# A four-layer graph network on one core: matmuls of zeros in TensorE's waits, records scattered in pairs, 39 row buffers, and a border that is merged

## The chip, the core and the metric

The kernel runs on one core of one Trainium2 chip, as one program. Times are microseconds of device time (us). The core's engines are TensorE (PE, with its weight loads as PEld), VectorE (DVE), ScalarE (ACT), GpSimd (POOL) and SyncE (SP). Each has a queue of its own and works in its order; they meet at semaphores. SP, ACT and POOL issue DMAs.

## What is computed

384 nodes with 512 features pass through four layers; each has a part on the graph (12,288 edges) and a part on the nodes, each added to its input:

```
x = x + L0_gnn(ln(x))   # softmax over a dense 8 x 384 x 384 matrix of edge weights, times values, elu, layer norm
x = x + L0_ffn(ln(x))   # each node's first expert by a gate, with gelu
x = x + L1_gnn(ln(x))   # 4 blocks: sparse attention by segments, then relu(y @ m_w1) @ m_w2
x = x + L1_ffn(ln(x))   # top-2 of 16 experts, 96 places each
x = x + L2_gnn(ln(x))   # graph attention: exp of a score per edge, sum of weighted rows by node
x = x + L2_ffn(ln(x))   # 8 experts mixed by a softmax
x = x + L3_gnn(ln(x))   # transformer attention on the graph
x = x + L3_ffn(ln(x))   # one of 3 attentions is chosen by argmax(relu(mean(x) @ r_w1 + b) @ r_w2 + b)
```

In L0 the weights are `softmax(mat)`, and `y = matmul(softmax(mat), x @ Wv + bv)` by head (8 heads of 64 columns). The tables of edges have to be sorted by node for L2, which is done once, on the chip.

## The kernel before

N = 384 nodes are NT = 3 tiles of P = 128 rows; D = 512 columns are KC = 4 chunks. Each engine has one hand-written queue: functions marked `@on("pe")`, `@on("dve")` and so on are run in the order of the text. No planner changes it. TensorE writes to eight banks of PSUM in turn: `banks.open` (line 54) waits until the bank's last user has freed it and gives the bank, `banks.filled` and `banks.drained` are the readers' and the writers' waits. A `mm` (line 372) of fp32 operands is two records of the trace.

The places that the change touches, in the order of time:

- **The bucket's start** (lines 893 to 902). TensorE turns the first rows (`l0x`), waits until they are drained, then for `bucket_ready` from VectorE, and multiplies two small triangles.
- **The softmax of L0** (lines 999 to 1030 on PE, 1073 to 1095 on ACT, 1403 to 1495 on DVE). `l0o0` to `l0o2` are the values, copied by ACT to `ost`. `totals` is a small matmul that DVE reads. `chunk_max_by_halves(2)` takes the row maxima of the last third of the matrix (`wm[2]`), after which ACT makes 24 exponentials (8 heads, 3 tiles), each with its row sum by `accum_out`. TensorE turns the weights of a head (line 1012, 9 transposes) and multiplies them with `ost`; `head_out` scales by the reciprocals of the sums.
- **The edges' scatter** (lines 2125 to 2135). POOL writes ST = 104 columns of records to `tab_sorted` by indirect DMAs, behind the banks `base0`, `base1`, ..., which TensorE fills during L1. `few_underway` (line 291) waits, before each, for the landing of the one two places ahead. TensorE, DVE and ACT work on the blocks of L1 meanwhile; their results meet at line 2061.
- **L1's experts** (lines 2184 to 2375). A gate (`f1g`), the count of places (`f1p1`, `f1n1`, `f1p2`), rows scattered to `tab_x`; ACT loads them group by group (`load_group`, 384 rows in one DMA), TensorE turns them (line 2248) and runs the 16 experts; DVE copies all results (line 2362), ACT stores them in `tab_eo`.
- **L2's start** (lines 2425 to 2445 on PE, 2500 to 2510 on ACT). Rows of `tab_eo` are gathered and added, normed (`act_row_std`), turned and multiplied.
- **The rows of L2.** POOL gathers 98 rows of 128 x 512 by `pool_scatter_rows` (line 629) to GR = 31 buffers, at most four underway. The first 31 are issued while the scores of the edges are made; then come the lanes (`lanes_ready` 1 to 5, small steps between DVE and PE), and then the sums, in which a buffer is free when TensorE has used it (`msg_used`).
- **L2's mixer, L3's choice and the end.** `f2g` (line 2713); `f3x`, the mean of each column by `accum_out` (line 3061), `f3r`, `f3g` and `q_taken`; after the last `f3y` one DMA of x to `out` by SP (line 3161), released by `out_ready`.

## Time and profile before

| | us |
|---|---|
| median of 3 runs | 1850.32 (1849.62 to 1850.44) |
| the profiled execution | 1841.83 |
| its span | 1840.1 |
| PE busy | 1601.8 (87%) |
| DVE, ACT, POOL busy | 886.2, 501.0, 645.1 |
| mean granted clock of TensorE | 0.925 |

The clock is given as a share of full speed: 1.00 is 2.4 GHz, 0.50 is 1.2 GHz. An engine that is busy for 87% of the span can still wait where others set the end, and part of its busy time is work at the lower clock. The chain of waits is the path that ended last, followed back.

### The profile page before, as it was taken

Reading aid. Unit: us, or ns where it says so; the run is one execution under the profiler, and the core shown is the slowest. Engines: PE = TensorE matmul, PEld = TensorE weight load, DVE = VectorE, ACT = ScalarE, POOL = GpSimd, SP = SyncE. Lnnn points to the kernel's source line nnn. Section 1 sums busy time; section 2 is a strip of 40 time slices with the busy share of each in tenths; the row PEclk is TensorE's granted clock in tenths of the full one; section 3 lists DMA queues with packets and bytes.
Section 4 is the critical chain, followed back from the end, with each engine's and each line's share of the span. In section 5 each row is a group of like instructions: output and inputs, shape, how many; then the busy total and the mean of one; then the engine's idle time right before and its main releaser. Section 6 shows DMA issues by size and latency. Waiting matters only on the chain.

```text
span 1840.1 us, 22730 instructions
## 1 busy us (share of the span) xinstructions
PE 1601.8 (87%) x6886; PEld 886.1 (48%) x6916; DVE 886.2 (48%) x2166; ACT 501.0 (27%) x1608; POOL 645.1 (35%) x756
## 2 busy tenths in 40 slices
PE   5989999997798999996995976488699899999698
PEld 3534444446454555463553745333244455555455
DVE  8878888887624524432353154576632101011322
ACT  1134444446422324141231214211110211111233
POOL 5867787862322335453002613457300000000000
PEclk9999999998698999997997886589899999999899
DMA  7021101007223132321216734346315122211020
GB/s 305 12 96 24 58 24 59 24 12 202 40 91 117 51 100 53 88 76 33 92 46 134 277 97 143 99 126 178 125 56 202 69 74 68 97 47 34 6 63 17
DMA packets 119547, 161.71 MB, mean 88 GB/s; under 512 B 49433, under 2 KB 61657, under 8 KB 119090
## 3 DMA queue, kind: packets, MB, share of 16 engines
q1 hardware_dynamic: 93024, 115.43, 20.2%
q0 software_dynamic: 18592, 29.91, 6.0%
q10 hardware_dynamic: 7858, 15.44, 2.5%
q8 instruction: 41, 0.67, 0.2%
q14 instruction: 32, 0.26, 0.1%
HBM read 145.26 MB, written 15.47 MB: 87 GB/s over the span
## 4 chain that ended last, share of the span: by engine, by line
PE 78%; DVE 12%; another core or an unknown queue 3%; issue 3%; ACT 2%; DMA 1%; POOL 0%; DVEq 0%; ACTq 0%; POOLq 0%
PE psum L373 76%; DVE stats L464 1%; DVE arena L2622 1%; DVE ring L1281 1%; PE psum L1012 1%; DVE xn L2042 1%; DVE xn L2048 0%; PE psum L2248 0%; DVE xn L2061 0%; DVE ring L656 0%; DVE mv L465 0%; PE psum L398 0%; DMA x<-in_x 0%; POOL tab_x L2291 0%
## 5 line engine op out<-in xcount | busy, mean ns | idle before, releaser
L373 PE MATMUL psum<-arena 128*128 128x128 f32 (+9 forms) x1814 | 328.9, 338 | 57.9 <-issue 31.7
L373 PE MATMUL psum<-arena,ring 128*128 (+1 forms) x1478 | 322.8, 363 | 9.0 <-issue 6.2
L373 PE MATMUL psum<-xT,ring 128*128 128x384 f32 x928 | 321.2, 508 | 9.8 <-ACT ring L3068 4.2
L373 PEld LDWEIGHTS psum<-arena 128*128 128x128 f32 (+5 forms) x1814 | 201.0, 157 | 191.7 <-issue 117.2
L373 PE MATMUL psum<-ring,arena 128*128 128x512 f32 (+1 forms) x592 | 273.4, 610 | 14.0 <-issue 6.6
L373 PE MATMUL psum<-ring,xT 128*128 128x512 f32 x552 | 250.5, 606 | 4.0 <-DMA bc<-in_wide 2.9
L373 PEld LDWEIGHTS psum<-xT,ring 128*128 128x128 f32 x928 | 183.2, 199 | 141.4 <-issue 31.4
L373 PEld LDWEIGHTS psum<-arena,ring 128*128 128x128 bf16 (+1 forms) x1504 | 139.2, 115 | 130.0 <-issue 28.6
L373 PEld LDWEIGHTS psum<-ring,arena 128*128 128x128 f32 (+1 forms) x592 | 103.4, 189 | 140.8 <-issue 139.4
L1063 ACT ACTIVATE ring<-ring 128x128 f32<-128x128 f32 x416 | 123.3, 297 | 173.1 <-DVE ring L1347 168.6
L373 PEld LDWEIGHTS psum<-ring,xT 128*128 128x128 f32 x552 | 104.3, 194 | 125.3 <-issue 119.9
L844 POOL DMA_INDIRECT tab_bucketed<-rec,pos x96 | 95.6, 996 | 186.2 <-DMA tab_bucketed<-rec,pos 178.3
L1347 DVE SCALAR_TENSOR_TENSOR ring<-psum,wa 128x1024 f32<-128x1024 f32 x104 | 127.4, 1225 | 59.5 <-PE psum L373 58.9
L2132 POOL DMA_INDIRECT tab_sorted<-rec,pos x104 | 100.4, 965 | 87.7 <-DMA tab_sorted<-rec,pos 62.0
L1155 POOL TENSOR_SCALAR arena<-iota,arena 128x128 bf16<-128x128 f32 x200 | 122.0, 619 | 15.0 <-DVE xT L1361 11.8
L1167 POOL DMA_INDIRECT tab_w<-xT,pair x104 | 109.9, 1057 | 49.2 <-DMA tab_w<-xT,pair 32.4
L408 ACT ACTIVATE arena<-psum 128x384 f32<-128x384 f32 (+1 forms) x133 | 63.6, 500 | 192.7 <-PE psum L373 154.1
L2061 DVE TENSOR_TENSOR xn<-xn,psum 128x512 f32<-128x512 f32 x24 | 16.5, 687 | 139.3 <-PE psum L373 106.4
L621 POOL DMA_INDIRECT ring<-tab_h,sd_t x72 | 74.6, 1037 | 24.7 <-issue 16.2
L482 ACT ACTIVATE std<-mv,eps_col 128x1 f32<-128x1 f32 x57 | 16.8, 294 | 227.9 <-DVE mv L465 203.6
L1063 ACT ACTIVATION_READ_ACCUMULATOR ring<-ring 128x1 f32 x416 | 77.6, 186 | 0.0
L1355 DVE TENSOR_REDUCE mask_dst<-ring 128x4 f32<-128x512 f32 x104 | 70.3, 676 | 0.0
(468 smaller groups left out, 1632.6 us busy)
## 6 DMA issues: line engine op xcount, KB each, us to landing
ring<-in_L_ffn_w SPq DMA_DIRECT2D x22, 1024.0 KB, 6.6
ring<-in_L_gnn_m_w SPq DMA_DIRECT2D x8, 1024.0 KB
ring<-in_L_ffn_expert_weights SPq DMA_DIRECT2D x8, 1024.0 KB
ring<-tab_key ACTq DMA_DIRECT2D x24, 256.0 KB
ring<-in_L_gnn_Wv SPq DMA_DIRECT2D x5, 1024.0 KB, 5.2
tab_w<-xn SPq DMA_DIRECT2D x6, 768.0 KB, 14.6
ring<-in_L_gnn_Ww SPq DMA_DIRECT2D x4, 1024.0 KB, 7.7
ring<-in_L_gnn_wq SPq DMA_DIRECT2D x4, 1024.0 KB, 5.8
```

Source lines behind the costliest of these rows:

```text
L373: return nc.tensor.matmul(o, a, b, start=start, stop=stop)
L408: nc.scalar.activation(dst, b[:, 0:w], ACT.Copy).then_inc(banks.free_of(name), 1)
L464: od.link(nc.vector.bn_stats(stats[:, t, :], src[:, t, :]))
L621: return nc.gpsimd.indirect_dma_start(o, None, table, bass.IndirectOffsetOnAxis(ap=column.bitcast(U32), axis=0), **more)
L844: nc.gpsimd.indirect_dma_start(tab_bucketed, bass.IndirectOffsetOnAxis(ap=pos[:, q:q + 1].bitcast(U32), axis=0), rec[:, q, :], None).then_ ...
L1012: last = nc.tensor.transpose(b[:, t * P:(t + 1) * P], weights_of(h, t)[:, c * P:(c + 1) * P], ident[:])
L1063: last = nc.scalar.activation(prod2[:, b % 2, h, :], prod2[:, b % 2, h, :], ACT.Copy, accum_out=w_sum[:, b, h:h + 1])
L1155: last = nc.gpsimd.tensor_scalar(edge_is[:, j, k, s_, :], iota[:, 0:P], key_rq[:, s_, T:T + 1], None, ALU.is_equal)
L1167: nc.gpsimd.indirect_dma_start(tab_w, bass.IndirectOffsetOnAxis(ap=pair[:, q:q + 1].bitcast(U32), axis=0), w_edge0[:, q, :], None).then_in ...
L1347: V.scalar_tensor_tensor(out=prod2[:, b % 2], in0=z_bank[:, b % 2], scalar=0.0, in1=wa_all, op0=ALU.max, op1=ALU.mult).then_inc(z_free, 1)
L1355: V.tensor_reduce(w_sum[:, b, 0:H8 // 2], prod2[:, b % 2, 0:H8 // 2, :], AX, ALU.add).then_inc(halves_summed, 1)
L2132: nc.gpsimd.indirect_dma_start(tab_sorted, bass.IndirectOffsetOnAxis(ap=pos2[:, q:q + 1].bitcast(U32), axis=0), rec[:, q, :], None).then_i ...
```

## The change

A function `keep_clock(b, n, w)` is added: n fp32 matmuls of a block of zeros (128 x w, w is 256 or 128), each into the bank b, which TensorE has opened and fills next, and whose content is overwritten. It is called 19 times, ahead of waits of TensorE, with counts of 3 to 22. Beside it:

- In L0 the totals' matmul moves ahead of `l0o2`, and `chunk_max_by_halves(2)` ahead of DVE's reading of the totals. `accum_out` goes from the exponentials; `ost` gets a column of ones for each head, so that the product's 65th column is the row sum; the reciprocal and its product move to `head_out`.
- SP waits for the landing of the halves of `wm[2]` before it loads the base rows.
- The scatter to `tab_sorted` waits for two landings before every second record (`OF_RECORDS` is 2), in place of one before each.
- The first group of `tab_x` comes in three DMAs and is turned tile by tile. The last 5 results of the 16 are copied by ACT, the first 11 by DVE, which then makes all of `l2_fold`.
- L2: ACT's order of stds and turned blocks; GR is 39 (the new buffers are parts of `xT`, `xT2` and `xn2`) with eight shared semaphores; during the first 39 rows POOL waits at every sixth for the landing of the four before.
- L3: the column means by 12 matmuls against ones in a bank `f3m` and a sum on DVE, ACT's four copies around `f3r`, their drain behind the choice.
- The output leaves in three DMAs, each behind its `f3y`.

The diff, without lines that only serve names (each hunk's head stands, its unchanged lines do not):

```diff
@@ -23,7 +23,7 @@
-GR = 31
+GR = 39
@@ -372,6 +372,10 @@
+        def keep_clock(b, n, w=256):
+            for _ in range(n):
+                mm(b[:, 512 - w:512], zeros[:, 0:P], zeros[:, 0:w], True, True)
+
@@ -596,9 +600,10 @@
-        ost = view(NT * N * H8, NT, D)
-        pw = view(NT * N * H8 + NT * D, 2, NT - 1, N)
-        pw_flat = view(NT * N * H8 + NT * D, N * H8 // 2)
+        ost = view(NT * N * H8, NT, H8 * (HD + 1)).rearrange("p t (h d) -> p t h d", h=H8)
+        after_ost = NT * N * H8 + NT * H8 * (HD + 1)
+        pw = view(after_ost, 2, NT - 1, N)
+        pw_flat = view(after_ost, N * H8 // 2)
@@ -607,6 +612,8 @@
+        go_rows += [v.rearrange("p c n -> p (c n)")[:, k * D:(k + 1) * D] for v, ks in ((xT, (0, 1, 2)), (xT2, (0, 2))) for k in ks]
+        go_rows += [xn2[:, t, :] for t in range(NT)]
@@ -621,10 +628,11 @@
+        ROW_GROUP = 6
-            earlier = 1 if T % GR < 2 * NT else RECORDS + ST // UN if T % GR >= GR - UN else 0
-            eng.wait_ge(rows_landed[T % GR], 16 * (earlier + T // GR + 1))
+            earlier = 1 if T % UN < 2 * NT else 0
+            eng.wait_ge(rows_landed[T % UN], 16 * (earlier + T // UN + 1))
@@ -632,9 +640,12 @@
-                if T >= ROWS_UNDERWAY:
+                if 0 < T < GR and T % ROW_GROUP == 0:
+                    for k in range(max(T - ROWS_UNDERWAY, 0), T):
+                        row_landed(pool, k)
+                elif T >= ROWS_UNDERWAY:
-                pool_gather(go_rows[T % GR], table, sd_t[:, T:T + 1]).then_inc(rows_landed[T % GR], 16)
+                pool_gather(go_rows[T % GR], table, sd_t[:, T:T + 1]).then_inc(rows_landed[T % UN], 16)
@@ -893,8 +904,9 @@
+            b = banks.open(pe, "bucket")
+            keep_clock(b, 6)
-            b = banks.open(pe, "bucket")
@@ -999,15 +1011,20 @@
-            pe.wait_ge(totals_ready, 1)
-            b = banks.open(pe, "totals")
-            mm(b[:, 0:NT], tri[:], node_total, True, True)
-            mm(b[:, 16:16 + NT], ones[:], node_total, True, True).then_inc(banks.full_of("totals"), 1)
+                if t == 1:
+                    pe.wait_ge(totals_ready, 1)
+                    b = banks.open(pe, "totals")
+                    mm(b[:, 0:NT], tri[:], node_total, True, True)
+                    mm(b[:, 16:16 + NT], ones[:], node_total, True, True).then_inc(banks.full_of("totals"), 1)
-                    pe.wait_ge(exp_done, h + 1)
+                    if h > 0:
+                        pe.wait_ge(exp_done, h + 1)
+                        if h == 0 and c == 0:
+                            keep_clock(b, 6)
+                            pe.wait_ge(exp_done, 1)
@@ -1073,8 +1090,7 @@
-                                            bias=gate[:, 5, t * H8 + h:t * H8 + h + 1],
-                                            accum_out=gate[:, 9, h * NT + t:h * NT + t + 1])
+                                            bias=gate[:, 5, t * H8 + h:t * H8 + h + 1])
@@ -1083,8 +1099,11 @@
-            for t in range(NT):
-                act_copy(act, f"l0o{t}", ost[:, t, :])
+            nc.scalar.activation(ost[:, :, :, HD], ones[:, 0:NT * H8].rearrange("p (t h) -> p t h", t=NT), ACT.Copy)
+            for t in range(NT):
+                b = banks.filled(act, f"l0o{t}")
+                nc.scalar.activation(ost[:, t, :, 0:HD], b.rearrange("p (h d) -> p h d", h=H8),
+                                     ACT.Copy).then_inc(banks.free_of(f"l0o{t}"), 1)
@@ -1423,11 +1442,11 @@
+            chunk_max_by_halves(2)
-            chunk_max_by_halves(2)
@@ -1461,9 +1480,11 @@
-                b = banks.filled(dve, f"l0y{h}")
-                V.tensor_tensor(xn2[:, :, h * HD:(h + 1) * HD], b[:, 0:NT * HD].rearrange("p (t d) -> p t d", t=NT),
-                                gate[:, 9, h * NT:(h + 1) * NT].unsqueeze(2).broadcast_to([P, NT, HD]),
+                b = banks.filled(dve, f"l0y{h}")[:, 0:NT * (HD + 1)].rearrange("p (t d) -> p t d", t=NT)
+                s3 = gate[:, 9, h * NT:(h + 1) * NT]
+                od.link(V.reciprocal(s3, b[:, :, HD]))
+                od.link(V.tensor_tensor(s3, s3, keep.rearrange("p (t h) -> p h t", h=H8)[:, h, :], ALU.mult))
+                V.tensor_tensor(xn2[:, :, h * HD:(h + 1) * HD], b[:, :, 0:HD], s3.unsqueeze(2).broadcast_to([P, NT, HD]),
@@ -1689,6 +1706,8 @@
+            sp.wait_ge(w_loaded[0], 32)
+            sp.wait_ge(w_loaded[NT - 1], 16)
@@ -1704,6 +1723,7 @@
+                keep_clock(bk["f0x"][0], *((14,) if t == 0 else (5, P)))
@@ -1875,8 +1895,12 @@
+                        if (k, i, c, t) == (0, 0, 0, 0):
+                            keep_clock(bk[0], 15, P)
+                if (k, i) == (0, 0):
+                    keep_clock(bk[0], 11, P)
@@ -2128,7 +2152,9 @@
-                few_underway(pool, q, RECORDS, OF_RECORDS)
+                if q >= OF_RECORDS and q % OF_RECORDS == 0:
+                    for k in range(q - OF_RECORDS, q):
+                        pool.wait_ge(ranks_landed[k % UN], 16 * (RECORDS + k // UN + 1))
@@ -2151,6 +2177,7 @@
+        ACT_RESULTS = 11
@@ -2184,6 +2211,10 @@
+            def load_first_group():
+                for t in range(NT):
+                    act.dma_start(xrows[:, t, :], tab_x[t * P:(t + 1) * P, :]).then_inc(first_group[t], 16)
+
@@ -2192,12 +2223,18 @@
+            def take_result(e):
+                act.wait_ge(results_stored[e % GE], 16 * (e // GE))
+                b = banks.filled(act, f"f1e{e}")
+                nc.scalar.activation(eo[0:CAP1, e % GE, :], b[0:CAP1, :], ACT.Copy).then_inc(banks.free_of(f"f1e{e}"), 1)
+                store_result(e)
+
-            load_group(0)
+            load_first_group()
@@ -2209,10 +2246,11 @@
-                if e >= 2:
+                if 2 <= e < ACT_RESULTS + 2:
-            for e in range(E1 - 2, E1):
-                store_result(e)
+                if e > ACT_RESULTS:
+                    take_result(e - 1)
+            take_result(E1 - 1)
@@ -2223,25 +2261,38 @@
-            def before(name, mask):
-
-                b = banks.open(pe, name)
+            def before(b, name, mask):
+
+            b = banks.open(pe, "f1p1")
+            keep_clock(b, 5)
-            before("f1p1", chosen_1)
+            before(b, "f1p1", chosen_1)
+            b = banks.open(pe, "f1p2")
+            keep_clock(b, 8)
-            before("f1p2", chosen_2)
+            before(b, "f1p2", chosen_2)
-                pe.wait_ge(group_in[g % 2], 16 * (g // 2 + 1))
+                if g == 0:
+                    bk = [banks.open(pe, f"f1t0{c}") for c in range(KC)]
+                    keep_clock(bk[0], 22)
+                    for t in range(NT):
+                        pe.wait_ge(first_group[t], 16)
+                        for c in range(KC):
+                            last = nc.tensor.transpose(bk[c][:, t * P:(t + 1) * P], xrows[:, t, c * P:(c + 1) * P], ident[:])
+                            if t == NT - 1:
+                                last.then_inc(banks.full_of(f"f1t0{c}"), 1)
+                    return
+                pe.wait_ge(group_in[g % 2], 16 * (g // 2 if g % 2 == 0 else g // 2 + 1))
@@ -2355,13 +2406,14 @@
-            for e in range(E1):
+            for e in range(ACT_RESULTS):
-                if E1 - GE - 1 <= e < E1 - 1:
-                    l2_fold(dve, od, e - (E1 - GE - 1))
+            for j in range(GE):
+                l2_fold(dve, od, j)
+            banks.filled(dve, f"f1h{E1 - 1}")
@@ -2429,6 +2481,7 @@
+            keep_clock(ends, 22)
@@ -2470,28 +2523,33 @@
-            pe.wait_ge(lanes_ready, 1)
+                if k == 0:
+                    keep_clock(b, 9)
+                    pe.wait_ge(lanes_ready, 1)
+            b = banks.open(pe, "l2m")
+            keep_clock(b, 6)
-            b = banks.open(pe, "l2m")
+            b = banks.open(pe, "l2w")
+            keep_clock(b, 3)
-            b = banks.open(pe, "l2w")
+                b = banks.open(pe, f"l2v{k}")
+                keep_clock(b, (6, 3)[k])
-                b = banks.open(pe, f"l2v{k}")
@@ -2500,8 +2558,11 @@
-            for t in range(NT):
+            act_row_std(act, ROW_L2, 0)
+            act_turned_block(act, "l2x", xT, 0)
+            for t in range(1, NT):
+            for t in range(1, NT):
@@ -2711,6 +2772,7 @@
+            keep_clock(logits, 13)
@@ -2983,10 +3045,22 @@
-            pe_transpose_rows(pe, "f3x", xn, 6 * NT)
+            bk = [banks.open(pe, f"f3x{c}") for c in range(KC)]
+            means = banks.open(pe, "f3m")
+            for t in range(NT):
+                if t == NT - 1:
+                    keep_clock(means, 7)
+                pe.wait_ge(row_ready, 6 * NT + t + 1)
+                for c in range(KC):
+                    last = mm(means[:, c * NT + t:c * NT + t + 1], xn[:, t, c * P:(c + 1) * P], ones[:, 0:1], True, True)
+                if t == NT - 1:
+                    last.then_inc(banks.full_of("f3m"), 1)
+                for c in range(KC):
+                    last = nc.tensor.transpose(bk[c][:, t * P:(t + 1) * P], xn[:, t, c * P:(c + 1) * P], ident[:])
+                    if t == NT - 1:
+                        last.then_inc(banks.full_of(f"f3x{c}"), 1)
-            for c in range(KC):
-                banks.drained(pe, f"f3x{c}")
+            banks.drained(pe, "f3m")
@@ -3016,12 +3090,16 @@
+            for c in range(KC):
+                banks.drained(pe, f"f3x{c}")
+            b = banks.open(pe, "f3q0")
+            keep_clock(b, 7)
-                pe_cols(pe, f"f3q{c}", xT, w, c * P)
+                pe_cols(pe, f"f3q{c}", xT, w, c * P, b=b if c == 0 else None)
@@ -3056,11 +3134,12 @@
-            for c in range(KC):
-                b = banks.filled(act, f"f3x{c}")
-                nc.scalar.activation(xT[:, c, :], b[:, 0:N], ACT.Copy, accum_out=route[:, c:c + 1]).then_inc(banks.free_of(f"f3x{c}"), 1)
+            for c in range(KC // 2):
+                act_copy(act, f"f3x{c}", xT[:, c, :], N)
+            for c in range(KC // 2, KC):
+                act_copy(act, f"f3x{c}", xT[:, c, :], N)
@@ -3102,6 +3181,8 @@
+            b = banks.filled(dve, "f3m")[:, 0:KC * NT].rearrange("p (c t) -> p c t", c=KC)
+            nc.vector.tensor_reduce(route[:, 0:KC], b, AX, ALU.add).then_inc(banks.free_of("f3m"), 1)
@@ -3157,9 +3235,10 @@
-            sp.wait_ge(out_ready, 1)
-            sp.dma_start(tiled(out), x[:]).then_inc(stored, 16)
-            sp.wait_ge(stored, 16)
+            for t in range(NT):
+                banks.drained(sp, f"f3y{t}")
+                sp.dma_start(out[t * P:(t + 1) * P, :], x[:, t, :]).then_inc(stored, 16)
+            sp.wait_ge(stored, 16 * NT)

```

On TensorE, at the start of the heads of L0, the order before (`gate,tri` is the totals, `ident,ring` a transpose of the first head):

```order
L373 MATMUL psum<-ring,xT 128x512 [waits bank_free2]
L373 MATMUL psum<-ring,xT 128x512 x3
L373 MATMUL psum<-rows,ones 128x512
L373 MATMUL psum<-gate,tri 128x3 [waits bank_free3,totals_ready]
L373 MATMUL psum<-gate,ones 128x3
L1012 MATMUL psum<-ident,ring 128x128 [waits bank_free4,exp_done]
L1012 MATMUL psum<-ident,arena 128x128 x2
L1012 MATMUL psum<-ident,ring 128x128 [waits bank_free5]
L1012 MATMUL psum<-ident,arena 128x128 x2
```

and now, from the second of the values on:

```order
L373 MATMUL psum<-ring,xT 128x512 [waits bank_free1]
L373 MATMUL psum<-ring,xT 128x512 x3
L373 MATMUL psum<-rows,ones 128x512
L373 MATMUL psum<-gate,tri 128x3 [waits bank_free2,totals_ready]
L373 MATMUL psum<-gate,ones 128x3
L373 MATMUL psum<-ring,xT 128x512 [waits bank_free3]
L373 MATMUL psum<-ring,xT 128x512 x3
L373 MATMUL psum<-rows,ones 128x512
L373 MATMUL psum<-zeros 128x256 [waits bank_free4]
L373 MATMUL psum<-zeros 128x256 x5
L1029 MATMUL psum<-ident,ring 128x128 [waits exp_done]
L1029 MATMUL psum<-ident,arena 128x128 x2
```

The totals stand ahead of the third `ring,xT`, and six products of zeros ahead of the wait for the exponentials.

On GpSimd, at the start of the scatter to the sorted table (`rec` are the records, `pos` their places), before:

```order
L2132 DMA tab_sorted<-rec,pos 26112x4 [waits bank_free7,sorted_cleared,bucketed_loaded]
L2132 DMA tab_sorted<-rec,pos 26112x4
L2132 DMA tab_sorted<-rec,pos 26112x4 [waits ranks_landed0]
L2132 DMA tab_sorted<-rec,pos 26112x4 [waits ranks_landed1]
L2132 DMA tab_sorted<-rec,pos 26112x4 [waits ranks_landed2]
```

and now:

```order
L2158 DMA tab_sorted<-rec,pos 26112x4 [waits bank_free7,sorted_cleared,bucketed_loaded]
L2158 DMA tab_sorted<-rec,pos 26112x4
L2158 DMA tab_sorted<-rec,pos 26112x4 [waits ranks_landed1,ranks_landed0]
L2158 DMA tab_sorted<-rec,pos 26112x4
L2158 DMA tab_sorted<-rec,pos 26112x4 [waits ranks_landed3,ranks_landed2]
```

Each record waited for one landing; now every second one waits for two, and the one behind it for none.

On TensorE, between L1's gate and its experts, before (`arena` in the transposes is the first group of rows):

```order
L373 MATMUL psum<-gate,tri_b 128x16 [waits bank_free2,step_ready]
L373 MATMUL psum<-gate,ones_b 128x16
L373 MATMUL psum<-gate,tri_b 128x16
L373 MATMUL psum<-gate,ones_b 128x16 x2
L373 MATMUL psum<-gate,tri_b 128x16
L2248 MATMUL psum<-ident,arena 128x128 [waits bank_free3,group_in0]
L2248 MATMUL psum<-ident,arena 128x128 x2
L2248 MATMUL psum<-ident,arena 128x128 [waits bank_free4]
```

and now:

```order
L373 MATMUL psum<-zeros 128x256 x7
L373 MATMUL psum<-gate,tri_b 128x16 [waits step_ready]
L373 MATMUL psum<-gate,ones_b 128x16
L373 MATMUL psum<-gate,tri_b 128x16
L373 MATMUL psum<-gate,ones_b 128x16 x2
L373 MATMUL psum<-gate,tri_b 128x16
L373 MATMUL psum<-zeros 128x256 [waits bank_free5,bank_free6,bank_free4,bank_free3]
L373 MATMUL psum<-zeros 128x256 x21
L2291 MATMUL psum<-ident,arena 128x128 [waits first_group0]
L2291 MATMUL psum<-ident,arena 128x128 x3
L2291 MATMUL psum<-ident,arena 128x128 [waits first_group1]
L2291 MATMUL psum<-ident,arena 128x128 x3
```

Ahead of each of the two waits stand products of zeros, and the transposes wait by tile for a load of their own.

## Rows read from the trace of the kernel before

**Rows 1.** Page, part 4: shares of the chain that ended last, by engine

```profile
PE 78%; DVE 12%; another core or an unknown queue 3%; issue 3%; ACT 2%; DMA 1%; POOL 0%; DVEq 0%; ACTq 0%; POOLq 0%
```

**Rows 2.** TensorE by stretch: start:end, length, busy us (instructions), granted clock, DMA share, GB/s

```profile
433.00:453.00 20.00, 20.00 (x185) 1.00 0.21 66
...
1014.00:1024.00 10.00, 8.88 (x44) 0.53 0.17 66
1093.90:1102.00 8.10, 7.32 (x17) 0.51 0.13 36
1118.00:1186.00 68.00, 38.97 (x564) 0.53 0.50 154
...
1746.30:1750.40 4.10, 4.08 (x7) 0.51 0.69 155
```

**Rows 3.** Three blocks of layer 1 by stretch: PE, PEld, DVE, ACT, POOL busy, clock

```profile
673.70:745.80 72.10, 70.35 (x257) 40.47 (x257) 29.07 (x58) 24.58 (x58) 36.61 (x38) 1.00 0.28 70
773.10:862.97 89.87, 72.95 (x257) 41.49 (x257) 29.17 (x59) 24.83 (x58) 45.44 (x47) 0.90 0.22 59
891.95:963.40 71.45, 70.05 (x256) 40.49 (x257) 29.07 (x58) 24.79 (x58) 0.00 (x0) 1.00 0.18 59
```

**Rows 4.** Chain of waits, 812 to 856 and 1100 to 1210: start, us, what

```profile
819.35 31.63 another core or an unknown queue
...
1131.12 7.89 another core or an unknown queue
```

**Rows 5.** GpSimd in time: start, us, line, operation, count [idle before it <-releaser]

```profile
641.42 0.96 POOL L844 DMA_INDIRECT tab_bucketed<-rec,pos  x1 [1.39 <-DMA tab_bucketed<-rec,pos]
...
818.32 0.96 POOL L2132 DMA_INDIRECT tab_sorted<-rec,pos  x1 [0.30 <-issue]
...
850.60 0.96 POOL L2132 DMA_INDIRECT tab_sorted<-rec,pos  x1 [0.30 <-issue]
```

**Rows 6.** All engines in time, 415 to 434

```profile
420.87 0.16 DVE L1427 COPY gate<-psum 128x3 f32<-128x3 f32 x1 [4.43 <-PE psum L373]
...
425.76 1.00 ACT L1075 ACTIVATE arena<-ring,gate 128x384 f32<-128x384 f32 x1 [3.68 <-DVE gate L1412]
...
427.88 0.47 PE L1012 MATMUL psum<-ident,ring 128*128 128x128 f32 x1 [7.04 <-ACT arena L1075]
```

**Rows 7.** TensorE in time, 10 to 24

```profile
16.58 0.17 PE L373 MATMUL psum<-gate,tri_b 128*128 128x9 bf16 x1 [3.49 <-DVE gate L1206]
```

**Rows 8.** What TensorE waited for: us in total, times, longest

```profile
PE psum L398 <- DVE xn L477: 15.5, 3, 12.7
PE psum L2248 <- DMA arena<-tab_x: 12.9, 1, 12.9
```

**Rows 9.** TensorE and ScalarE in time, 1093 to 1108

```profile
1100.03 1.99 PE L373 MATMUL psum<-ring,xT 128*128 128x512 f32 x2
...
1101.99 1.10 PE L373 MATMUL psum<-ring,xT 128*128 128x512 f32 x2
...
1105.42 0.66 PE L398 MATMUL psum<-ident,xn 128*128 128x128 f32 x4 [1.72 <-DVE xn L477]
...
1104.24 0.28 ACT L482 ACTIVATE std<-mv,eps_col 128x1 f32<-128x1 f32 x1
```

**Rows 10.** GpSimd's gathers of rows in time, first and last of 67

```profile
1208.91 1.14 POOL L621 DMA_INDIRECT arena<-tab_h,sd_t  x1 [30.67 <-PE psum L373]
...
1303.41 0.95 POOL L621 DMA_INDIRECT arena<-tab_h,sd_t  x1 [0.30 <-issue]
```

**Rows 11.** All engines in time, 1729 to 1747

```profile
1739.60 1.84 PE L373 MATMUL psum<-route,ring 128*128 128x1 f32 x8 [1.65 <-ACT xT L3061]
...
1746.32 0.98 PE L373 MATMUL psum<-xT,ring 128*128 128x384 f32 x1 [4.22 <-ACT ring L3068]
```

**Rows 12.** The output's DMA (issue to landing), and the chain at a store of 192 KB

```profile
DMA to landing us min/median/max: 3.5/3.5/3.5
...
1082.67 2.06 DMA tab_eo<-arena
```

18 lines of the change are left out of this document (6 added, 12 removed).

## The prediction

> **What bounds the kernel now.** I read the chain of waits first: TensorE is 78% of it, VectorE 12%, and "another core or an unknown queue" 3% [rows 1], which on one core should be nothing and has to be explained. Then TensorE by stretch, for the granted clock: 0.53 of full speed in the experts' first transposes, 0.51 behind the gathers of L2's start, 0.53 through all 68 us in which L2's edges are scored [rows 2]. In each of these the engine had waited for others just before, or waits often. So the time is set by TensorE's work, by its waits, and by the work that runs at 1.2 GHz behind a wait. What a cold stretch costs can be read: a pair of 128x512 records lasts 1.99 us at the low clock and 1.10 at the full one [rows 9], and since the records of a pair overlap, a product of zeros of 256 columns costs half of what a 512-column product takes from start to start, near 0.45 us at full clock and 0.85 at half.
>
> The unknown 3% comes next. Three blocks of layer 1 hold the same work, but take 72.1, 89.9 and 71.5 us [rows 3]. In the long one the chain has a piece of 31.63 us of unknown from 819.35 on [rows 4], while VectorE waits for a product of TensorE. Exactly then GpSimd issues its scatters without a pause, one per 1.27 us from 818.32 to 850.60 [rows 5]; the piece ends at 850.98. In the third block GpSimd does nothing and no such piece exists. My reading: TensorE's signal reaches the waiting engine only when GpSimd's run of indirect DMAs has ended.
>
> **The change part by part.** All against the profiled execution's own 1841.8 us.
>
> *Scatter in pairs.* Each pair now ends with a wait for the later landing. Where GpSimd waited for the DMA just issued, starts lay about 2.36 us apart (0.96 of issue and 1.39 of idle time) [rows 5], and the chain has no unknown piece there. A pair then takes 1.27 + 2.36 = 3.6 us against 2.5, and the run is cut into pieces of 1.3 us. If a signal gets through in each pause, the middle block falls from 89.9 to 72, which is -17.9; I take -16, for some delay remains. The scatter's end moves: 104 records at 1.8 us are 189 us, about what it took, and the 27 left at 818 need 49 us and not 34, to 867. Its reader, the load of the sorted table, is a layer later. Bounds -18 and +12, the second if a signal still waits for the whole run, now 15 us longer.
>
> *L0's softmax.* VectorE is idle for 4.43 us ahead of the totals at 420.87 [rows 6]. The maximum of the last third moves there, so the exponentials no longer wait for VectorE (3.68 us in the same rows) but for ACT's own copies, some 1 us more: the start of the heads, 427.88, moves 3 us. Its first 5 us run at the low clock; six products of zeros (2.7 us, of a gap of 7.04) keep it up, worth about 2.5. Against that stand a 65th column and, behind the last head, a reciprocal and a product, +1.3. Sum -4.2, bounds -5.5 and -1.
>
> *The bucket's keep_clock.* This stands after the drain of `l0x`, at about 13.6, and TensorE is cold: 6 x 0.85 = 5.1 us reach to 18.7, where the product started at 16.58 [rows 7]. VectorE's long chain waits for it: +2.2, bounds 0 and +2.3. It is the one place where the zeros are longer than the wait.
>
> *L1's experts.* The transposes waited 12.9 us for their load [rows 8]; then 10 us ran at 0.53 [rows 2]. Twenty-two products are 9.9 us at full clock and fit; cold they would be 18.7 and late by 6. Five and eight products stand before it and bring the clock up, the first of them ending about 1 us late. With full clock 10 us at 0.53 lose 4.4 us, and turning tile by tile leaves a third of the transposes behind the last landing, another 1. With the late start: -3, bounds -6 and +6.
>
> *L1's end and L2's start.* Results 11 to 15 leave by ACT, with no `l2_fold` in front: 0.6 us earlier. The wait of 12.7 us [rows 8] takes 22 products of zeros (9.9 us), and 8.1 us at 0.51 behind it [rows 2] lose up to 3.5. The third std stood behind a copy, at 1104.24, so TensorE waited 1.72 us at 1105.42 [rows 9]; in the new order it doesn't. Up to -5.8; I take -4, bound +6 as above.
>
> *Rows of L2.* Between the first and last of 67 gathers lie 94.5 us, 1.43 each [rows 10]; TensorE waits for them here. Eight rows more are there beforehand: 8 x 1.43 = 11.5. What falls away turns cold TensorE at the end. But eight rows (1.25 each, as [rows 5]) and some four pauses of up to 2.4 lengthen GpSimd's part in the scoring by up to 20 us, beside which VectorE and TensorE exchange signals; there a run of eight gathers had an unknown piece of 7.89 us [rows 4], and runs are now cut at six. I set both at nothing and take -9 for the rows. Bounds -16 and +8.
>
> *L3's choice.* ACT's four copies with their sums lay ahead of the route's product: it waited 1.65 us and ran cold for 1.84 [rows 11]; now only a sum on VectorE lies there: -2.3. Seven products of zeros fill 3 of the 4.22 us before 1746.32 [rows 11], and 4.1 us at 0.51 [rows 2] become 2.1. -4, bounds -5 and -2.
>
> *The output.* A DMA of 768 KB took 3.5 us to land; one of 192 KB 2.06 [rows 12]. The last third, with the hop over VectorE's memset gone: -1.1. The Trainium skill, DMA: Bandwidth & Descriptors, "Anatomy of one DMA", fits 2.0 us plus bytes over 436 GB/s: 3.8 and 2.6 us by it, so the term would be -1.4.
>
> *The other zeros* (f0x, the first rows of layer 1, the lanes, `f2g`): each returns half of some 4 to 5 us of cold work if it fits its wait. I take -4.7 for all, bounds -10 and +3.
>
> Sum: -16 - 4.2 + 2.2 - 3 - 4 - 9 - 4 - 1.1 - 4.7 = -43.8. That gives 1798.0 on the profile's scale. The profiled execution lay 8.5 below the median of the runs, so the median should be 1806.5.
>
> One rule speaks against the zeros in L0. In the rows the clock is full through the later heads, 433 to 453 [rows 2], though a third of each head's time is transposes. The Trainium skill, TensorE: Matmul & The Clock Gate, "PE-mode transpose", says that transposes don't count as busy for the gate. By it the clock could fall again inside the heads, and the term would be 2.5 less; the trace doesn't bear that out.
>
> **The rivals.**
> - *The stall stays.* Pairs of issues might hold signals as runs do, the pause of about 1.4 us being too short; the two unknown pieces above don't show which pause frees them. The term -16 becomes 0: 1822. For it: the scoring stage has such pieces with runs of only eight; against it: none stood where single scatters had pauses.
> - *The zeros run cold.* The clock is down where they start, so they take twice as long: the two blocks of 22 end 6 us late each, and the gains at full clock (some 14 us) go. -43.8 + 25 gives 1831. For it: the clock before the experts' wait was low already. Against: five and eight products stand before the first of the two, and in [rows 9] the clock came back within unbroken work.
> - *Slower: signals are held for all of GpSimd's issuing, paused or not.* Then the longer scatter costs 12 and doesn't save 16 (+28), and 39 rows with pauses, ending near 1198, hold the lanes that began at 1186 (+12) and add some 6 to the scoring: 1806.5 + 46 = 1852. It decides at one point: whether TensorE's signals pass in a pause of one landing.
> - *More than forecast.* Cutting the gathers at six also frees the scoring, where the unknown pieces such as that of 7.89 sum to about 20: half of it gives 1796.
>
> **How the numbers follow.** The forecast 0.56; the stall stays 0.14; zeros cold 0.10; slower 0.08; more than forecast 0.12. The range, 1787 to 1836, leaves out the slower case and the tails of the outer two. A measurement of this kernel can tell about 0.2% (3.7 us) from no change. Faster by more: 0.90; within: 0.03; slower: 0.07, nearly all from the third rival, whose lower half would lie within.
>
> **What would show it.** The middle block of layer 1 at about 72 us, with no unknown piece near 820; if there is one as long as the scatter, the first or third rival holds. The granted clock near 1.00 behind the two waits of 12 us, and the zeros there at 0.43 to 0.47 each; at 0.85 the second. The bucket's product at about 18.7. The heads of L0 from 425. Gathers after the lanes: 59, with the same spacing. The forecast is wrong if the scoring stage grows beyond its 68 us, or if the rows' last gather comes no earlier relative to the lanes.

## The result, and the profile after

The changed kernel takes 1805.09 us (median of 4 runs, 1804.19 to 1807.99), the kernel before 1849.97 (4 runs, 1843.08 to 1850.44): a ratio of 0.9769, with a 95% interval of 0.9743 to 0.9794. Faster, by 2.3%. The profiled execution of after took 1805.19 us, so it lies on its median, where that of before (1841.83) lay 8.1 below the median of its four. Trace against trace the gain is 36.6 us, and 44.9 by the medians.

TensorE's busy time rose, though the span fell (page of after, part 1):

```profile
PE 1656.8 (92%) x7256; PEld 940.3 (52%) x7286; DVE 880.0 (49%) x2161; ACT 501.5 (28%) x1586; POOL 645.3 (36%) x756
```

55 us more. The new products (173, two records each) are nearly all of a group of 362 records and 89.7 us; other work got shorter at the full clock (group of the page: line, engine, form, count | busy, mean ns | idle before).

```profile
L373 PE MATMUL psum<-zeros 128*128 128x256 f32 (+3 forms) x362 | 89.7, 409 | 14.6 <-ACT cnt_dst L412 4.0 <-issue 3.1 <-DVE arena L2674 2.5
```

The three blocks of layer 1, by stretch (columns as in [rows 3]). The middle one takes 69.8 us in the place of 89.9; each stretch holds the same work, in 252 to 258 matmul records:

```profile
667.60:739.70 72.10, 70.68 (x258) 40.97 (x259) 29.74 (x59) 25.44 (x60) 26.96 (x28) 1.00 0.27 70
766.40:836.20 69.80, 69.14 (x252) 40.05 (x252) 27.42 (x56) 24.19 (x56) 28.43 (x30) 1.00 0.25 68
865.20:936.70 71.50, 70.08 (x257) 40.54 (x257) 29.19 (x58) 24.84 (x58) 27.23 (x28) 1.00 0.20 64
```

GpSimd in time, from 817 on (to be read against [rows 5]): two scatters 1.26 us apart, then 1.87 us of waiting.

```profile
817.96 0.96 POOL L2158 DMA_INDIRECT tab_sorted<-rec,pos  x1 [1.88 <-DMA tab_sorted<-rec,pos]
819.22 0.96 POOL L2158 DMA_INDIRECT tab_sorted<-rec,pos  x1 [0.30 <-issue]
822.05 0.96 POOL L2158 DMA_INDIRECT tab_sorted<-rec,pos  x1 [1.87 <-DMA tab_sorted<-rec,pos]
```

Not all of these waits are so short: in the middle block there are 14, of 2.6 us on average. And the wait of VectorE that was the piece of 31.63 us before now takes 14.0 us. "Remote" is the profile's word for a wait that ended long after the last recorded instruction that could have ended it. (VectorE in time, before; then what GpSimd and VectorE waited for in the middle block, after.)

```profile
851.01 0.69 DVE L2061 TENSOR_TENSOR xn<-xn,psum 128x512 f32<-128x512 f32 x1 [31.66 <-remote]
```

```profile
POOL tab_sorted L2158 <- DMA tab_sorted<-rec,pos: 36.8, 14, 4.9
...
DVE xn L2085 <- PE psum L373: 14.4, 3, 14.0
```

So some 14 of the 31.6 us were TensorE's own work on the product, and some 17.7 the lateness of its signal.

Start of L0's heads and the bucket's product, in time (for [rows 6] and [rows 7]). The zeros of L0 run from 422.20, 12 records in 2.86 us, and the first transpose starts at 425.85; those of the bucket took 2.83:

```profile
13.55 2.83 PE L373 MATMUL psum<-zeros 128*128 128x256 f32 x12 [0.67 <-ACT xT L412]
16.27 0.18 PE L373 MATMUL psum<-gate,tri_b 128*128 128x9 bf16 x1
...
422.20 2.86 PE L373 MATMUL psum<-zeros 128*128 128x256 f32 x12
...
425.85 0.33 PE L1029 MATMUL psum<-ident,ring 128*128 128x128 f32 x1 [0.80 <-ACT arena L1092]
```

TensorE's waits from 985 to 1110 (for [rows 8]): that for the loads of `tab_x` is 1.7 us and not 12.9. Behind both long waits the clock is now full (TensorE by stretch, columns as in [rows 2]), but it is 0.54 in the scoring, as before:

```profile
PE psum L2291 <- DMA arena<-tab_x: 1.7, 2, 1.0
...
986.00:996.00 10.00, 7.23 (x57) 1.00 0.41 129
1062.20:1070.30 8.10, 6.54 (x30) 1.00 0.15 47
1084.60:1151.00 66.40, 40.90 (x534) 0.54 0.50 152
```

And the place where the gain did not come. What VectorE waited for in the sums, 1165 to 1292, and the chain there:

```profile
DVE arena L652 <- PE psum L373: 16.7, 8, 7.8
DVE arena L652 <- remote: 15.1, 1, 15.1
...
1242.95 15.06 another core or an unknown queue
...
1283.93 6.66 another core or an unknown queue
```

The two pieces are not alike. Ahead of the end of the first, TensorE is idle for 13.58 us while GpSimd issues gathers to 1254.76: that is a late signal. In the second TensorE works without a pause to 1290.35, and GpSimd issues nothing: that is TensorE's own work, though the profile finds no releaser for its end. (GpSimd and TensorE in time.)

```profile
1254.76 0.95 POOL L628 DMA_INDIRECT ring<-tab_h,sd_t  x1 [0.30 <-remote]
...
1259.98 2.07 PE L373 MATMUL psum<-xT,arena 128*128 128x512 f32 x2 [13.58 <-DVE xT L667]
...
1290.17 0.18 PE L373 MATMUL psum<-arena 128*128 128x24 bf16 x1
```

Something is lost between the two as well, ahead of the lanes. VectorE's result for them was done at 1145.62, but the nine products of zeros, begun at 1144.26 at little more than half clock, kept TensorE from its transposes until 1151.12. VectorE waited 6.63 us for these, and 2.10 in the kernel before (TensorE and VectorE in time, after; VectorE, before):

```profile
1144.26 7.02 PE L373 MATMUL psum<-zeros 128*128 128x256 f32 x18 [2.51 <-DVE arena L2674]
...
1151.12 1.04 PE L2533 MATMUL psum<-ident,arena 128*98 128x128 f32 x8
...
1152.26 0.42 DVE L2701 TENSOR_TENSOR_SCAN arena<-arena,psum 98x128 f32<-98x128 f32 x1 [6.63 <-PE psum L2533]
```

```profile
1188.98 0.42 DVE L2640 TENSOR_TENSOR_SCAN arena<-arena,psum 98x128 f32<-98x128 f32 x1 [2.10 <-PE psum L2478]
```

The same instructions of VectorE in both traces, one against the other, tell how the gain builds up:

| stretch, by time of before | forecast | traces |
|---|---|---|
| bucket and the loop behind it, to 406 | +2.2 | +1.5 (-0.3 at the bucket) |
| L0's softmax, 406 to 462 | -4.2 | -4.3 |
| the other zeros, 462 to 795, and f2g | -4.7 with the lanes | -3.8 |
| scatter, 795 to 955 | -16 | -20.0 |
| L1's experts, 961 to 1027 | -3 | -3.1 |
| experts' end and L2's start, 1027 to 1105 | -4 | -6.3 |
| scoring, lanes and sums, 1105 to 1324 | -9 | +2.3 |
| L3's choice, 1728 to 1783 | -4 | -1.3 |
| output | -1.1 | -1.7 |
| sum | -43.8 | -36.7 |

Within the row of +2.3 the scoring gave -5.1, the lanes +4.1 and the sums +3.3. Of the +1.5 in the first row, 1.4 arise between 51 and 99 us, in the loop behind the bucket; no run shows from what.

### The profile page after: what moved, and what is told of

Same layout as the page of the kernel before. It is cut to its first block and busy times, and to the rows that moved or that the text cites. A ratio compares the mean times of both kernels' runs of the same rounds, so it can differ in the third digit from the quotient of the medians.

```text
span 1803.5 us, 23480 instructions
## 1 busy us (share of the span) xinstructions
PE 1656.8 (92%) x7256; PEld 940.3 (52%) x7286; DVE 880.0 (49%) x2161; ACT 501.5 (28%) x1586; POOL 645.3 (36%) x756
## 5 line engine op out<-in xcount | busy, mean ns | idle before, releaser
L373 PE MATMUL psum<-arena 128*128 128x384 f32 (+9 forms) x1804 | 321.0, 334 | 34.2 <-issue 14.8
L373 PE MATMUL psum<-xT,ring 128*128 128x384 f32 x928 | 312.7, 498 | 6.3 <-ACT xT L412 4.2
L373 PE MATMUL psum<-ring,arena 128*128 128x512 f32 (+1 forms) x570 | 259.2, 604 | 4.9 <-ACT arena L2947 3.8
L373 PEld LDWEIGHTS psum<-xT,ring 128*128 128x128 f32 x928 | 179.3, 195 | 133.2 <-issue 19.9
L373 PE MATMUL psum<-ring,xT 128*128 128x512 f32 x552 | 246.0, 597 | 1.8 <-DMA bc<-in_wide 0.8
L373 PEld LDWEIGHTS psum<-ring,arena 128*128 128x128 f32 (+1 forms) x570 | 99.3, 187 | 126.6 <-issue 125.5
L1174 POOL TENSOR_SCALAR arena<-iota,arena 128x128 bf16<-128x128 f32 x200 | 122.3, 620 | 16.5 <-DVE xT L1380 13.6
L373 PE MATMUL psum<-zeros 128*128 128x256 f32 (+3 forms) x362 | 89.7, 409 | 14.6 <-ACT cnt_dst L412 4.0
L373 PEld LDWEIGHTS psum<-zeros 128*128 128x128 f32 (+1 forms) x365 | 71.3, 216 | 30.2 <-issue 11.3
```

Source lines behind the costliest of these rows:

```text
L373: return nc.tensor.matmul(o, a, b, start=start, stop=stop)
L1174: last = nc.gpsimd.tensor_scalar(edge_is[:, j, k, s_, :], iota[:, 0:P], key_rq[:, s_, T:T + 1], None, ALU.is_equal)
```

## The experiments

Theory A is that of the prediction: while GpSimd issues indirect DMAs in a row, signals of other engines arrive late. The kernel before was run beside every variant. It took two quite different times. In the first two groups of runs (e1 to e4, e8) it took 1775 us, in the others (e9 to e12) 1845, near the 1850 on record. So each variant is read against the kernel before of its own group, and I call the first the quiet condition and the second the holding one. Three more runs were meant for this question, the two kernels again and the kernel before with the pairs alone (e5 to e7); they gave no time. So the pairs were tested only by undoing them in the changed kernel.

### e1: one landing before each scatter

```diff
-                if q >= OF_RECORDS and q % OF_RECORDS == 0:
-                    for k in range(q - OF_RECORDS, q):
-                        pool.wait_ge(ranks_landed[k % UN], 16 * (RECORDS + k // UN + 1))
+                few_underway(pool, q, RECORDS, OF_RECORDS)
```

> The changed kernel with one part undone: the scatter to the sorted table waits again for one landing before each record. Theory A (TensorE's signals are held while GpSimd issues indirect DMAs without a pause): the middle block of layer 1 has its unknown piece of some 30 us again, and takes 88 to 92 us instead of 71; time 1805 + 20 = 1825 (1819 to 1828). Rival B (the block's gain comes from the zeros or from another place and time of the scatter): the block stays at 72 and the time within 3 us of 1805.

Measured: 1765.99 us, 0.9948 (0.9931 to 0.9965) of the kernel before, which took 1774.96. Neither theory had that time; the block stayed, as rival B had it. GpSimd issued up to 17 scatters in a row, with at most 0.62 us between them (808.72 to 829.67), and yet the chain there is TensorE's and the block takes 69.8 us (GpSimd in time; the block by stretch; the chain):

```profile
820.52 0.96 POOL L2156 DMA_INDIRECT tab_sorted<-rec,pos  x1 [0.30 <-issue]
821.79 0.96 POOL L2156 DMA_INDIRECT tab_sorted<-rec,pos  x1 [0.30 <-issue]
...
767.00:836.80 69.80, 69.10 (x251) 40.03 (x252) 27.48 (x56) 24.23 (x56) 37.25 (x39) 1.00 0.23 65
...
811.92 22.25 PE psum L373 x88
```

In the kernel before the run was longer, 27 scatters from 816.76 on, but signals were late from 825.5 on, 9 us into it. So a run of this length is not enough; something that differs between the two conditions has to be there too. This trace says what the stage costs without it.

### e2: no products of zeros

```diff
         def keep_clock(b, n, w=256):
-            for _ in range(n):
-                mm(b[:, 512 - w:512], zeros[:, 0:P], zeros[:, 0:w], True, True)
+            return
```

> The changed kernel with no products of zeros at all. If the zeros give what their cold stretches cost: L0's heads start cold again (+2.5), the f0x and first rows of layer 1 +3, the experts' first transposes +4, L2's start +3.5, lanes +1, mixer and L3's choice +2 together, so 1805 + 16 = 1821 (1815 to 1826). If the zeros give little because they fit the wait badly (in the changed kernel's trace the last seven, ahead of q, ran at half clock and ended 2.4 us after q was ready): under 1812, and in L3's choice itself faster by 1 to 3 us than with them.

Measured: 1773.38 us, 0.9988 (0.9978 to 0.9999); the changed kernel in the quiet condition (e8) takes 0.9952. All the zeros together are worth 6 us in this condition, not 16. (e8 is of another group and chip, with the same 1774.96 beside it; in the holding condition the kernel without zeros wasn't run.) By instructions of VectorE, e2 against e8: L0 -1.6, the first rows of layer 1 -2.7, the experts +0.4, the start of L2 and the lanes -3 (all of it given back in the sums, which wait for rows there), L3's choice -3.2. The clock did come up (TensorE, two stretches without and with zeros):

```profile
565.00:590.00 25.00, 22.89 (x64) 0.83 0.17 58
...
1675.00:1690.00 15.00, 10.27 (x35) 0.63 0.49 107
```

```profile
565.00:590.00 25.00, 23.40 (x75) 1.00 0.23 61
...
1671.00:1686.00 15.00, 13.62 (x59) 1.00 0.50 112
```

### e3: pauses in the sums too

```diff
-                if 0 < T < GR and T % ROW_GROUP == 0:
+                if 0 < T and T % ROW_GROUP == 0:
```

> The changed kernel with a pause at every sixth gather of a row also in the sums (so far only in the first 39). Theory A: VectorE's wait of 15.09 us in the sums is a signal held by GpSimd's run of gathers; with pauses it goes, the sums take 100 to 106 us instead of 121, and the time is 1805 - 15 = 1790 (1787 to 1796). Rival C (the sums are limited by the pace of the gathers, as in the kernel before): ten more pauses of 2 us make them longer, 1805 to 1820.

Measured: 1799.33 us, 1.0121 (1.0092 to 1.0151): slower than the kernel before. In the quiet condition there is nothing to free, and the pauses cost time: VectorE waits for rows in the sums, and the last gather starts at 1281.3, not 1246.7 as in e8 (waits, 1172 to 1292):

```profile
DVE ring L667 <- DMA ring<-tab_h,sd_t: 31.7, 24, 4.2
```

Rival C is borne out for this condition. In the holding one it wasn't tried.

### e4: 31 row buffers

```diff
-GR = 39
+GR = 31
...
-        go_rows += [v.rearrange("p c n -> p (c n)")[:, k * D:(k + 1) * D] for v, ks in ((xT, (0, 1, 2)), (xT2, (0, 2))) for k in ks]
-        go_rows += [xn2[:, t, :] for t in range(NT)]
```

> The changed kernel with 31 row buffers instead of 39 (pauses at every sixth of the first 31 kept). The prediction's price: 8 x 1.43 = 11.5 less, some cold start: 1805 + 9 = 1814. By the trace of the changed kernel, in which the 39 rows saved nothing in the sums (-37.1 us where the sums start, -33.8 where they end): 1800 to 1807, no later end of the sums.

Measured: 1759.87 us, 0.9917 (0.9887 to 0.9946), the fastest in this condition. From the first gather to the end of the sums it takes 159.8 us, e8 with 39 buffers 164.4. More buffers gained nothing there. Whether they lose some 5 us is not clear (the intervals of e4 and e8 overlap), nor is why.

### e8: the changed kernel in the same condition

From here on SP's two waits against a count carry a check of that count, with no other edit here:

```diff
-                sp.wait_ge(w_landed, nc.values_load(landings[0:1, t:t + 1], engines=[mybir.EngineType.SP], min_val=16, max_val=16 * ST,
-                                                    skip_runtime_bounds_check_because="a count of tiles held between 1 and ST, times 16"))
+                sp.wait_ge(w_landed, nc.values_load(landings[0:1, t:t + 1], engines=[mybir.EngineType.SP], min_val=16, max_val=16 * ST))
```

> The changed kernel itself, on the chip of its variants if it is the same one (SP's two waits for a number of landings now check that number, two short instructions each on SP, early in the kernel). The chip of the first four variants showed no unknown piece in any chain, and the kernel before took 1775 us there and not 1850. Theory A with the addition that a chip may not hold signals: where it doesn't, the change gains little, 1758 to 1768 against 1775; where it does, 1805 against 1850. Rival D (the chip is only faster throughout): 0.977 of the kernel before, whatever that takes.

Measured: 1767.36 us, 0.9952 (0.9936 to 0.9967) against 1774.96. So where nothing is held the change is worth 8 us, not 45. e1 and e8 give the same time within 2 us: the pairs are worth nothing there. In the scoring VectorE waits 1.2 us for TensorE and never for a late signal (waits, 1089 to 1122):

```profile
DVE arena L2673 <- PE psum L373: 1.2, 2, 0.8
```

This trace also has the longest run of all: 62 gathers, at most 0.7 us between them (the first and the last):

```profile
1161.94 1.04 POOL L628 DMA_INDIRECT xn<-tab_h,sd_t  x1 [3.50 <-DMA xT<-tab_h,sd_t]
...
1246.69 1.10 POOL L628 DMA_INDIRECT ring<-tab_h,sd_t  x1 [0.30 <-issue]
```

In these 85 us no wait of any engine is marked remote. The same holds up to 1320 us in all five quiet traces (e1 to e4, e8), while each of the six holding ones (before, after, e9 to e12) has such waits. Rival D falls by the ratio, 0.9952 and not 0.977. Rival E, other spacings of GpSimd's issues, falls too: they lie 1.25 to 1.27 us apart in both conditions.

### e9: the kernel before, traced again

Its only edit is the one on SP's count.

> The kernel before, for its trace on this chip. Theory A with its addition (this chip doesn't hold signals): the middle block of layer 1 takes 72 us and not 90, though GpSimd issues its scatters in a row there; the scoring of the edges about 45 and not 68; no unknown piece in the chain; the span near 1773. Rival E (GpSimd's indirect DMAs are spaced or land otherwise here, so that there is no run): the spacing of the scatters from 818 on isn't 1.27 us.

It fell in the holding condition: 1850.93 us, the kernel before beside it 1844.61 (1819 to 1857). So it doesn't show the quiet kernel before, but it shows the pieces again, in the same places and of other sizes (chain, 640 to 990): 24.53 us at 822.25 and 11.40 at 850.08.

```profile
822.25 24.53 another core or an unknown queue
...
850.08 11.40 another core or an unknown queue
```

The first piece ends at 846.78, where GpSimd goes on issuing every 1.27 us to 858.90. So the prediction's reading, that a signal gets through "only when GpSimd's run of indirect DMAs has ended", is too strong: signals are late in a run, but some arrive within it.

### e10: 31 buffers, no pauses, four products ahead of q

```diff
-                if 0 < T < GR and T % ROW_GROUP == 0:
-                    for k in range(max(T - ROWS_UNDERWAY, 0), T):
-                        row_landed(pool, k)
-                elif T >= ROWS_UNDERWAY:
+                if T >= ROWS_UNDERWAY:
...
             b = banks.open(pe, "f3q0")
-            keep_clock(b, 7)
+            keep_clock(b, 4)
```

(with the edit of e4)

> The changed kernel with 31 row buffers, without pauses in the first rows, and with 4 products of zeros ahead of q instead of 7. Where signals aren't held (kernel before 1775): the pauses buy nothing and each costs GpSimd some 2 to 3 us, so the rows are there earlier and the scoring and sums are as fast as with pauses or faster: 1754 to 1760, of it 1 from the zeros ahead of q. Where they are held (kernel before 1850): the scoring has its unknown pieces of 5 to 8 us as in the kernel before, 1803 to 1812.

Measured in the holding condition: 1807.69 us, 0.9783 (0.9732 to 0.9834), beside 0.9769 for the change. The 39 buffers and the pauses at six together are worth nothing that can be measured there either. Scoring takes 64.5 us (first gather to last reduction; 65.0 in the kernel before), with waits for late signals of 29.7 us (VectorE's waits, 1087 to 1153):

```profile
DVE arena L2668 <- remote: 29.7, 7, 7.8
```

### e11: one landing before each scatter, again

The edit is that of e1.

> Again the changed kernel with one landing before each scatter in place of the pairs, in case the chip is one that holds signals (kernel before 1840 to 1855). Theory A there: the middle block of layer 1 has its unknown piece of 25 to 32 us again and takes 88 to 92 us, the time is 1805 + 20 = 1825 (1819 to 1830). Rival B: the block stays at 72. On a chip that doesn't hold them (kernel before 1775): 1766 as before.

Measured in the holding condition: 1827.42 us, 0.988 (0.9823 to 0.9938) of 1844.83. That is theory A's number; the block, which was expected at 88 to 92, takes 93.8 us where the changed kernel has 69.8, with unknown pieces in the chain (the block; the chain from 640 to 990):

```profile
766.40:860.20 93.80, 72.78 (x261) 42.04 (x260) 30.56 (x61) 26.37 (x61) 50.10 (x52) 0.88 0.21 59
...
813.27 16.92 another core or an unknown queue
...
833.48 7.26 another core or an unknown queue
...
844.04 10.71 another core or an unknown queue
```

One edit, undone in both conditions: it costs 22 us against the changed kernel on record in one (20 by the ratios, each to the kernel before of its own group), and nothing in the other. Within the holding condition the traces part cleanly. In the three with one landing before each scatter (before, e9, e11) VectorE's waits marked remote between 640 and 990 sum to 32.7, 36.0 and 35.0 us; in the three with pairs (after, e10, e12) there are none.

### e12: 31 buffers, pauses at every third row

```diff
-        ROW_GROUP = 6
+        ROW_GROUP = 3
```

(with 31 buffers and four products ahead of q)

> The changed kernel with 31 row buffers, pauses at every third gather of the first 31 instead of every sixth, and 4 products of zeros ahead of q. Theory A on a chip that holds signals: each run of gathers is 3.75 us and each pause lets the signals through, so the waits of VectorE marked remote in the scoring (25.0 us in the changed kernel) fall to about half, scoring from 60 to 45 or 50 us; the rows end 15 us later, which costs some 5 in the sums: 1795 to 1803. Rival F (the holding goes by how many gathers are issued in all, not by the length of a run): scoring stays at 60 and the time is 1805 to 1815. On a chip that doesn't hold them: scoring stays at 32, rows later, 1762 to 1772.

Measured in the holding condition: 1796.74 us (1794.93 to 1798.86), 0.9769 (0.9692 to 0.9846) of 1844.83, which spread widely; e11 beside it took 1827.42. Its own four runs lie below all four of the changed kernel (1804.19 to 1807.99), but those were taken in another group. Scoring falls to 44.7 us, from 59.5 with pauses at six and 64.5 with none; the waits for late signals go from 25.0 and 29.7 to 11.4 us (VectorE's waits in the scoring of the changed kernel, then of e12):

```profile
DVE arena L2674 <- remote: 25.0, 7, 5.3
```

```profile
DVE arena L2671 <- remote: 11.4, 6, 2.9
...
DVE arena L650 <- remote: 23.4, 1, 23.4
```

What is saved is partly lost again: the sums, whose gathers still run without a pause, have one such wait of 23.4 us. Rival F falls: it isn't how many gathers are issued in all. Whether the length of a run counts or how densely the gathers stand, these runs don't tell apart, since pauses at three change both.

## Why the prediction was right, and where it was not

**The scatter** was the step that carried the forecast, and it is shown: the block at 69.8, no unknown piece in it, and 22 us back in e11 when the edit is undone. The size was 20.0 where I had -16: I had kept a rest of delay that didn't remain, and the block by itself takes 69.8 us, not 72. The scatter's own end I had wrong, without a cost in the table: the last record was issued at 928.8, not 867, for the waits between pairs were 2.6 us on average and not 1.4. What the argument lacked was a condition. I read the third block, without scatters and without a stall, as proof that a run of scatters makes the stall; e1 has a run of 17 and no stall, e8 one of 62 gathers. The rival "the stall stays" asked whether a pause is long enough; nobody asked whether there is a stall each time. In the quiet condition the forecast would have failed: the change is worth 8 us there.

**L0's softmax** (-4.2, measured -4.3), **L1's experts** (-3, -3.1) and **L2's start** (-4, -6.3) came about as worked out, the last of them beyond the 5.8 that I had named as its most; no run shows where that rest comes from. In the experts it was for another reason than I gave: e2 shows that the zeros gave nothing there (+0.4), so by exclusion the 3 us are the loads by tile and the transposes that no longer stand behind the last landing; that wasn't tested by itself. The first five products start at half clock, 4.61 us for their ten records, and end some 1.4 us after what they wait for is there. L0's zeros were worth 1.6 us (e2), not 2.5. The clock stayed at 1.00 through the heads (426 to 448 us), so the rule of the Trainium skill on transposes (TensorE: Matmul & The Clock Gate, "PE-mode transpose") isn't what took the rest.

**The bucket** (+2.2): its premise, a low clock at 13.6 us, did not hold in the trace on record: in the changed kernel's trace the 12 records took 2.83 us, full clock, and the product started at 16.27. In five later traces (e1, e3, e4, e10, e12) it started at 18.1 to 18.8, as I had worked out, but L0's heads came only 0.8 to 1.3 us later than in e8 in four of them (4.8 in e3), where the product was 1.6 to 2.1 late. The chain behind it is not as tight as I took it to be.

**The rows of L2** (-9, measured +2.3) is the step that failed. It was this one: "Eight rows more are there beforehand: 8 x 1.43 = 11.5." They were: the last gather came 48.7 us earlier than before, the first of all 35.8, so 12.9 were gained between them. But earlier rows didn't shorten the sums, which got 3.3 us longer. GpSimd issued 30 gathers in a row to 1254.76, VectorE waited 15.06 us for a late signal, and TensorE stood idle for 13.58 of them (the rows of the result). The step took the rows' pace for the only thing that ends the sums. Late signals in the scoring it weighed and set at nothing; in the sums it had no term for them. That the eight buffers lengthened the run isn't shown: the longest runs in the sums are 26 and 27 gathers with 31 buffers in the two traces of the kernel before, 28 and 32 with 31 buffers in e10 and e12, and 30 and 33 with 39 in the changed kernel and e11. In the kernel before VectorE had late signals in the sums as well (17.7 us of waits), but they are not on its chain, where the rows set the pace.

The lanes took another 4.1 us, by the nine products of zeros that ran late; e10 has the same, less so (VectorE waits 4.7 us there). The prediction called the bucket "the one place where the zeros are longer than the wait"; the lanes are a second. In the quiet condition nobody waits for these zeros (e8: they end at 1127.9, and VectorE's result is ready at 1129.9), no signal is late, and rows set the pace by their landings (e3).

**L3's choice** (-4, measured -1.3): the mean by matmul worked, the route's product started 34.5 us earlier and needed 1.00 us, not 1.84. Then seven products of zeros ahead of q ran at half clock, 6.11 us for 14 records, and q started at 1713.47 though its weights were ready at 1711.06: 2.4 us late (TensorE, then ScalarE in time):

```profile
1707.52 6.11 PE L373 MATMUL psum<-zeros 128*128 128x256 f32 x14 [0.71 <-ACT xT L412]
...
1710.00 1.06 ACT L3147 ACTIVATE ring<-ring 128x1024 f32 x1 [2.52 <-DVE route_i L3197]
...
1713.47 1.78 PE L373 MATMUL psum<-xT,ring 128*128 128x384 f32 x5
```

That is my second rival, here, ahead of the lanes and at the experts' first five. From the route's product to q it is 8.32 us there, 5.95 in e8 where the same seven ran at full clock, 6.75 without zeros (e2), and 5.95 with four, in e10 and in e12.

**The output** (-1.1, -1.7): each DMA of 256 KB lands in 2.0 us (the source line's DMAs in after, for [rows 12]). From [rows 12] alone, 3.5 less 2.06, the term would have been near -1.4 before the hop; the -1.1 was too small. The estimate by the Trainium skill's fit (DMA: Bandwidth & Descriptors, "Anatomy of one DMA") was 2.6; the page gives that fit for DMAs issued by GpSimd, while SP issues these, and the measurement decides.

```profile
DMA to landing us min/median/max: 2.0/2.0/2.0
```

**The total.** 1806.5 was forecast and 1805.1 measured, but that is better than its steps were. By traces the sum was 7.2 us too large: the rows alone missed by 11.3, and the scatter gave 4 back. And the profiled execution of before lay some 8 below its median while that of after lies on it. That the two cancel is luck, and so is the condition: both kernels were timed in the holding one, where most of the gain is. The range from 1787 to 1836 was wide enough for either.

## What to carry to other kernels

Where an engine waits for a semaphore whose owner has long been done, look at what GpSimd issues at that time: its signal can be late during a run of indirect DMAs, and a wait for the landings after every second issue (2.6 us on average here, 4.9 at most) took that away at little cost, as long as GpSimd isn't what sets the pace. A wait marked as unknown is not all lateness: look at when the owner finished its work. Rows that come earlier help only as long as nothing else ends the wait. Zeros in a wait are worth half of the cold work behind it at most; sized close to the wait they can end late when the clock is down; at the one place tried, four did what seven did. And run the kernel before in more than one session: here the largest gain depended on it.

## What the runs showed that I had not expected

The same kernel took 1775 us in two groups of runs and 1845 in two others, the one steady (1772 to 1780 in 32 runs), the other less so (1819 to 1857 in 20), and the two conditions differ in one thing that the traces show: signals that come late while GpSimd issues in a row. It isn't the chip alone: e1 to e4 (quiet) and e11 and e12 (holding) ran on the same one; e8 ran on a second, e9 and e10 on a third. What sets the condition stays open; the runs don't show it. The changed kernel, in 1805 us (on record) and in 1767 (e8), shows where it counts: its first gather stands at 1084.6 and 1089.2 us, so all of the difference comes behind it. The stage from the first gather of a row to the end of the sums shows its size: 191 to 209 us in the holding condition (before, after, e9 to e12), 160 to 166 in the quiet one (e1, e2, e4, e8), but for e3's 196 with its added pauses.

In the holding condition the times also vary more (e11: 1801.69 to 1839.26 in 10 runs; e8: 1758.31 to 1772.46), which fits pieces whose size depends on which signal falls into a run. That was not tested by itself.
